# Folding the FFN weight preparation into the first FFN pass, with weights stored block by block, in a Mamba + FFN + attention layer on eight cores

## The chip, the cores and the metric

The kernel runs on the eight cores of one Trainium2 chip. Each core takes one of eight sequences (2048 tokens, 1024 features) and all weights; the cores exchange nothing. The metric is device microseconds of the slowest core. The engines of a core are PE (matmul; PEld is its weight load), DVE (vector), ACT (scalar/activation), POOL (GpSimd) and SP, which here only issues DMAs. SPq and POOLq are the queues on which they are issued.

## What is computed

The reference, cut to its skeleton (`_layernorm` without scale; every block is added to the residual):

```python
x = x + mamba(_layernorm(x))      # in_proj, conv, silu, x_proj, dt, scan over time, out_proj
x = x + ffn(_layernorm(x))
x = x + attn(_layernorm(x))
x = x + ffn(_layernorm(x))        # the same w1, w2, b1, b2 again

def _binarize(w):                 # w1 is [4096, 1024], w2 is [1024, 4096]
    alpha = mean(abs(w), axis=1, keepdims=True)
    return alpha * sign(w)
def ffn(x):
    h = gelu(einsum('bsd,hd->bsh', x, _binarize(w1)) + b1)
    return einsum('bsh,dh->bsd', h, _binarize(w2)) + b2
```

So both FFN calls need the sign of each weight and, for each output feature, the mean of the absolute weights (alpha).

## The kernel before

The residual X stays in SBUF, features on partitions (8 chunks of 128) and tokens along the free dimension. The program is written by hand: a recorder keeps one list of operations for each engine (`r.op`), waits stand in these lists in program order (`r.wait`), `r.drain` lets the engine finish, `r.inc` is a drain and a semaphore increment, and `r.barrier` joins all engines. An engine that waits holds up all that stands behind it in its list.

- **Mamba** (`_mamba`), four quarters of 512 tokens. In quarter 0 `inproj_block` loads each of 32 blocks of in_proj_w by POOL with a cast to bf16 (L443, 128 columns of the matrix, so runs of 512 B), multiplies (L472, 8 matmuls), and SP writes the bf16 block to `ip_bf` in HBM (L448, runs of 256 B). The load of block m waits for the matmuls and for the write of block m-2, which use the same of two buffers. Quarters 1 to 3 load the block from `ip_bf` (L459); of these, the first 16 blocks are placed between the channel groups of the scan before, the last 16 follow the output projection. `do_outproj` does the same with 8 blocks of out_proj_w (L585, L593, L602; matmuls L611, residual add L618). The scan (L712 ACT exponentials, L726 and L750 DVE products, L734 DVE scan) fills most of the stage and isn't touched.
- **Preparation** (`_ffn_prep`), between two barriers. A first pass over w1 (32 blocks of 128x1024, loads L843) and w2 (8 blocks of 128x4096) takes the sums of absolute values on DVE (L847) and scales them (L852) into `al1_t`, `al2_t`. A second pass loads the transposed weights w1T, w2T in column blocks (L872, runs of 512 B), takes the sign on ACT (L879, f32 to bf16) and writes the result to `w1s`, `w2s` in HBM (L885, runs of 256 B).
- **FFN** (`_ffn`, called twice), each time two halves of 1024 tokens. A half is a layer norm (L298 to L343; its sums over features are f32 and bf16 matmuls with a matrix of ones, L308 and L313); then 32 blocks of the first product: load of a w1s block (L925), 16 matmuls (L936), GELU on ACT with alpha as its scale (L943), with two weight buffers and two PSUM pairs; then 8 blocks of the second product: load of a w2s block (L955, 1 MB), 64 matmuls (L966), alpha and bias on DVE (L973), residual add (L980); then a barrier.
- **Attention** (`_attn`): over the 16 heads of one token, in 16 groups of 128 tokens; not touched.

## Time and profile before

| | us |
|---|---|
| Times of two runs | 6597.5 and 6752.1, median 6674.8 |
| The profiled execution | 6606.3 |
| Span of its slowest core (core 6), on which all rows below are | 6604.8 |
| Spans of the other cores | 6568.6 to 6604.1 |
| Mean granted TensorE clock, every core | 0.66 of full speed |

| Stage on core 6 | from | to | us |
|---|---|---|---|
| start, x and first layer norm | 0 | 101 | 101 |
| Mamba, in-projection of quarter 0 | 101 | 248 | 147 |
| rest of Mamba | 248 | 3583 | 3335 |
| preparation of the FFN weights | 3583 | 4094 | 511 |
| FFN, first call, first half | 4094 | 4385 | 291 |
| FFN, first call, second half | 4385 | 4678 | 293 |
| attention | 4678 | 6010 | 1332 |
| FFN, second call, and the store | 6010 | 6605 | 595 |

A profile row gives busy times of each engine; PEclk is the clock that was granted to TensorE, 1.0 being 2.4 GHz and 0.5 being 1.2 GHz. The profile models the ends of matmuls, so a busy PE is not PE at its peak.

### The profile page before, as it was taken

How to read it: one execution, taken by the hardware profiler on the slowest of the kernel's cores; microseconds unless marked ns; L12 is line 12 of the kernel's file. 1: busy time of each engine (PE TensorE's matmuls, PEld its weight loads, DVE VectorE, ACT ScalarE, POOL GpSimd, SP SyncE). 2: the span in 40 equal slices, each digit the busy share in tenths (PEclk: the TensorE clock that was granted, in tenths of full speed). 3: DMA queues.
4: the chain of work that ended last, by engine and by line, in shares of the span. 5: the costliest groups of instructions: out<-in, count | busy, mean ns of one | idle time of the engine just before them, and what ended most of it. 6: DMA issues, size and time to landing. Idle time of an engine off the chain costs nothing.

```text
span 6604.8 us, 35054 instructions; the slowest of 8 cores (6568.6 to 6604.8 us)
## 1 busy us (share of the span) xinstructions
PE 2579.8 (39%) x8941; PEld 937.6 (14%) x9120; DVE 3260.0 (49%) x3060; ACT 1439.0 (22%) x2794; POOL 330.1 (5%) x124
## 2 busy tenths in 40 slices
PE   3333224232242232322222001879543343337978
PEld 1100001000010000100000000334211111113433
DVE  0267783577845778658885300120356556552011
ACT  0133331233322333223331012212110010011120
POOL 0000000000000000000000000000022322220000
PEclk8655557555575555665556555989766666668989
DMA  6500004100020000110002555323300000002414
GB/s 104 84 10 13 2 0 77 34 13 5 0 51 33 11 8 0 32 45 0 0 0 82 188 127 140 67 42 76 56 0 0 0 0 0 0 2 35 79 42 111
DMA packets 691332, 259.70 MB, mean 39 GB/s; under 512 B 614586, under 2 KB 680253, under 8 KB 687552
## 3 DMA queue, kind: packets, MB, share of 16 engines
q1 hardware_dynamic: 627488, 235.25, 14.6%
q0 software_dynamic: 63648, 22.20, 3.1%
q8 instruction: 78, 1.28, 0.1%
q14 instruction: 118, 0.97, 0.1%
HBM read 241.73 MB, written 37.88 MB: 42 GB/s over the span
## 4 chain that ended last, share of the span: by engine, by line
DVE 35%; PE 27%; DMA 12%; ACT 11%; issue 9%; DVEq 4%; POOL 1%; ACTq 1%; SPq 1%; POOLq 0%
DVE AR L734 18%; PE ps L966 7%; PE ps L936 6%; ACT AR L712 5%; DVE AR L1102 4%; PE ps L472 3%; DVEq L58 3%; DVE AR L1138 3%; PE ps L1165 2%; DVE AR L513 2%; DMA AR<-w1T 2%; PE ps L308 2%; PE ps L1069 2%; DMA AR<-w2T 2%; DMA AR<-w 2%
## 5 line engine op out<-in xcount | busy, mean ns | idle before, releaser
L758 PE MATMUL ps<-AR 128*128 128x512 bf16 x1004 | 510.2, 609 | 1945.7 <-DVE AR L750 1945.7
L734 DVE TENSOR_TENSOR_SCAN AR<-AR 128x1024 bf16<-128x1024 f32 x512 | 1173.5, 2292 | 135.4 <-ACT AR L718 124.0
L712 ACT ACTIVATE AR<-AR 128x511 f32<-128x511 f32 x1024 | 675.3, 707 | 1.4 <-issue 1.1
L936 PE MATMUL ps<-AR 128*128 128x512 bf16 x2008 | 455.1, 384 | 127.0 <-DVE AR L343 111.4
L1165 PE MATMUL ps<-AR 128*128 128x512 bf16 x512 | 220.5, 587 | 636.4 <-POOL AR L1151 609.2
L973 DVE TENSOR_SCALAR AR<-ps,AR 128x1024 f32<-128x1024 f32 x32 | 43.0, 1344 | 859.5 <-PE ps L966 859.5
L966 PE MATMUL ps<-AR 128*128 128x512 bf16 x2007 | 445.3, 382 | 16.3 <-DMA AR<-w2s 14.0
L308 PE MATMUL ps<-X,AR 128*128 128x512 f32 x256 | 133.9, 683 | 737.3 <-ACT AR L298 663.9
L750 DVE TENSOR_TENSOR AR<-AR 128x1024 bf16<-128x1024 bf16 x512 | 354.4, 692 | 125.3 <-issue 125.3
L758 PEld LDWEIGHTS ps<-AR 128*128 128x128 bf16 x1024 | 69.8, 104 | 2376.7 <-issue 2376.7
L743 ACT ACTIVATE AR<-AR 128x2 f32<-128x2 bf16 x512 | 105.0, 205 | 1351.3 <-DVEq L63 1351.3
L472 PE MATMUL ps<-AR 128*128 128x512 bf16 x1004 | 319.7, 481 | 160.3 <-DVE AR L343 66.0
L726 DVE TENSOR_TENSOR AR<-AR 128x1022 bf16<-128x1022 bf16 x512 | 351.1, 686 | 10.7 <-issue 10.7
L1151 POOL TENSOR_TENSOR AR<-AR 128x2048 bf16<-128x2048 bf16 x64 | 279.4, 4366 | 969.9 <-DVE AR L1124 878.5
L1138 DVE TENSOR_TENSOR AR<-AR 128x2048 bf16<-128x2048 bf16 x64 | 219.3, 3426 | 188.3 <-PE ps L1165 186.8
L322 DVE TENSOR_TENSOR AR<-AR 128x1024 f32<-128x1024 f32 (+1 forms) x10 | 10.1, 1013 | 590.5 <-ACT AR L318 590.5
L1102 DVE TENSOR_REDUCE AR<-AR 128x32 f32<-128x2048 bf16 x128 | 292.9, 2288 | 9.4
L1095 DVE TENSOR_TENSOR AR<-AR 128x2048 bf16<-128x2048 bf16 x128 | 155.7, 1217 | 250.8 <-ACT AR L1082 250.8
L936 PEld LDWEIGHTS ps<-AR 128*128 128x128 bf16 x2048 | 197.5, 99 | 384.7 <-issue 171.3
L966 PEld LDWEIGHTS ps<-AR 128*128 128x128 bf16 x2048 | 201.4, 98 | 260.2 <-issue 22.4
L943 ACT ACTIVATE AR<-ps,AR 128x1024 bf16<-128x1024 f32 x128 | 154.2, 1205 | 292.8 <-PE ps L936 292.7
L1069 PE MATMUL ps<-AR 128*128 128x512 bf16 x737 | 184.2, 389 | 71.7 <-ACT AR L1082 40.5
(92 smaller groups left out, 2176.2 us busy)
## 6 DMA issues: line engine op xcount, KB each, us to landing
AR<-w1s SPq DMA_DIRECT2D x128, 256.0 KB, 3.0
AR<-w2s SPq DMA_DIRECT2D x32, 1024.0 KB, 7.0
AR<-ip_bf SPq DMA_DIRECT2D x96, 256.0 KB, 2.9
AR<-bc_hbm SPq DMA_DIRECT2D x4, 4096.0 KB, 14.7
AR<-w SPq DMA_DIRECT2D x32, 512.0 KB, 3.4
AR<-w SPq DMA_DIRECT2D x8, 2048.0 KB, 9.3
AR<-w1T SPq DMA_DIRECT2D x32, 512.0 KB, 4.3
AR<-w2T SPq DMA_DIRECT2D x8, 2048.0 KB, 13.9
```

The source lines that it names most:

```text
L472: c = r.op("pe", lambda e, m=m, b=b, k=k: e.matmul(self.bank(4 + b, TQ), wi[b][:, k, :], xn[:, k, :], start=(k == 0), stop=(k == 7)), inc= ...
L712: nbase=nbase: e.activation(out=dec_all[gb][:, n, 1:TQ], in_=dt[b][:, 1:TQ], func=AF.Exp, scale=av[:, dd, nbase + n:nbase + n + 1]))
L726: e.tensor_tensor(out=inp_all[ib][:, :, 1:], in0=vdup[b][:, :, 1:], in1=bbc[:, nbase:nbase + G, 1:], op=ALU.mult))
L734: e.tensor_tensor_scan(out=h_all[hb].rearrange("p a b -> p (a b)"), data0=dec_all[gb].rearrange("p a b -> p (a b)"), data1=inp_all[ib].rea ...
L750: e.tensor_tensor(out=hc_all[hb], in0=h_all[hb], in1=cbc[:, nbase:nbase + G, :], op=ALU.mult), inc="c_ve")["c_ve"]
L758: e.matmul(self.bank(b, TQ), self.ident[:], hc_all[hb][:, n, :], start=(ng == 0 and n == 0), stop=(ng == NG - 1 and n == G - 1)),
L936: e.matmul(self.pair(4 + 2 * b, TH)[:, a:bnd], w1b[b][:, k, :], xn[:, k, a:bnd], start=(k == 0), stop=(k == 7)),
L966: e.matmul(self.pair(0 + 2 * b, TH)[:, a:bnd], w2b[b][:, k, :], hact[:, k, a:bnd], start=(k == 0), stop=(k == 31)),
L1069: e.matmul(self.pair(4)[0:U, ns * 512:(ns + 1) * 512], xn[:, k, m::16], wt[:, k, ns * 512:(ns + 1) * 512], start=(k == 0), stop=False))
L1102: cv = r.op("ve", lambda e, b=b, jg=jg, jb2=jb2: e.reduce_sum(out=sc[b][0:U, :, 2 * jg:2 * jg + 2].transpose([0, 2, 1]), in_=ot[jb2][0:U], ...
L1138: e.tensor_tensor(out=ot[jb][0:U], in0=vm[b][0:U, 2 * jg:2 * jg + 2, :].unsqueeze(2) .broadcast_to([U, 2, 16, 64]), in1=am[b][0:U, :, 2 * ...
L1165: ns=ns: e.matmul(self.bank(2 * b + ns)[0:U, :], self.ident[0:U, 0:U], ot[jb][:, jj, :, :] .rearrange("p a b -> p (a b)") [0:U, ns * 512:( ...
```

## The change

1. `_ffn_prep` is not called any more. The first call of `_ffn` gets `first=True`, and in its first half (`prep`) it does the preparation itself. For each of the 32 blocks of the first product: SP loads the f32 block of w1 into `sg1`; ACT takes the sign into `w1b` (bf16), drains, and takes the absolute value in place; PE forms the alpha of the 128 output features with 8 f32 matmuls whose stationary operand is the 128x128 block of absolute values and whose moving operand is one column of `onesf` (1/1024); SP writes `w1b` to `w1s`; then come the 16 matmuls as before; ACT copies alpha out of PSUM, drains, and does the GELU.
2. The second product takes w2 in half blocks in all halves (16 of 128x2048 where 8 of 128x4096 were; 32 matmuls for each). In the first half of the first call each half block is loaded in f32, goes through sign and absolute value on ACT, 16 f32 one-column matmuls, and a write to `w2s`. After the second half block ACT copies alpha out of PSUM, and DVE waits for that.
3. The host hands over copies of w1, w2, in_proj_w and out_proj_w in which every 128-column block lies contiguously in the order of the SBUF tile (`w1pk`, `w2pk`, `ip_pk`, `op_pk`), and `w1s`, `w2s`, `ip_bf`, `op_bf` are laid out likewise. So each partition's part of a block is one run (in_proj_w 4 KB, `ip_bf` 2 KB, out_proj_w 8 KB, `op_bf` 4 KB, w1 4 KB, w2 8 KB for each half block).
4. The scratch of the FFN layer norm lies on the place of `hact`.

The core of the diff:

```diff
         self._load_x()
         if "mamba" in self.stages:
             self._mamba()
-        if "prep" in self.stages:
-            self._ffn_prep()
         if "ffn1" in self.stages:
-            self._ffn()
+            self._ffn(first=True)
...
                 ddone = r.op("gp", lambda e, m=m, b=b: e.dma_start(
-                    out=wi[b], in_=d["in_proj_w"][:, m * 128:(m + 1) * 128]
-                    .rearrange("(k p) f -> p k f", p=128)),
+                    out=wi[b].rearrange("p a b -> p (a b)"),
+                    in_=d["ip_pk"][m * 128:(m + 1) * 128, :]),
...
         for hh in range(2):
+            prep = first and hh == 0
...
             for m in range(32):
                 b = m % 2
                 if m >= 2:
                     r.wait("sp", "c_pe", mm_done[m - 2])
+                if prep:
+                    if st_done[b]:
+                        r.wait("sp", dsem("sp", b), st_done[b])
+                    ddone = r.op("sp", lambda e, m=m, b=b: e.dma_start(
+                        out=sg1[b].rearrange("p a b -> p (a b)"),
+                        in_=d["w1pk"][m * 128:(m + 1) * 128, :]),
+                         inc=dsem("sp", b), inck=16)[dsem("sp", b)]
+                    r.wait("act", dsem("sp", b), ddone)
+                    ...
+                    r.op("act", lambda e, b=b: e.sign(out=w1b[b],
+                                                      in_=sg1[b]))
+                    r.drain("act")
+                    r.op("act", lambda e, b=b: e.activation(
+                        out=sg1[b], in_=sg1[b], func=AF.Abs))
+                    ab_done[b] = r.inc("act", "c_act")
+                    r.wait("pe", "c_act", ab_done[b])
+                    for k in range(8):
+                        r.op("pe", lambda e, m=m, b=b, k=k: e.matmul(
+                            self.bank(0, 512)[:, m:m + 1], sg1[b][:, k, :],
+                            self.onesf[:, 0:1], start=(k == 0),
+                            stop=(k == 7)))
+                    r.wait("sp", "c_act", ab_done[b])
+                    st_done[b] = r.op(
+                        "sp", lambda e, m=m, b=b: e.dma_start(
+                            out=d["w1s"][m * 128:(m + 1) * 128, :],
+                            in_=w1b[b].rearrange("p a b -> p (a b)")),
+                        inc=dsem("sp", b), inck=16)[dsem("sp", b)]
...
                 mm_done[m] = c["c_pe"]
                 r.wait("act", "c_pe", mm_done[m])
+                if prep:
+                    r.op("act", lambda e, m=m: e.activation(
+                        out=self.al1_t[:, m:m + 1],
+                        in_=self.bank(0, 512)[:, m:m + 1], func=AF.Copy))
+                    r.drain("act")
                 ev_done[m] = r.op("act", ... func=AF.Gelu, scale=self.al1_t[:, m:m + 1], ...
...
             for m in range(8):
+                bm = m % 2
+                for h in range(2):
+                    sb = 2 * m + h
+                    b2 = sb % 2
+                    k0 = 16 * h
+                    if sb >= 2:
+                        r.wait("sp", "c_pe", m2_done[sb - 2])
+                    if prep:
+                        ... load of sg2[b2] from w2pk by SP; ACT waits for it ...
+                        r.op("act", lambda e, b2=b2: e.sign(out=w2h[b2],
+                                                            in_=sg2[b2]))
+                        r.drain("act")
+                        r.op("act", lambda e, b2=b2: e.activation(
+                            out=sg2[b2], in_=sg2[b2], func=AF.Abs))
+                        ab2 = r.inc("act", "c_act")
+                        r.wait("pe", "c_act", ab2)
+                        for k in range(16):
+                            r.op("pe", ... e.matmul(
+                                     self.bank(4, 512)[:, m:m + 1],
+                                     sg2[b2][:, k, :], self.onesf[:, 0:1], ...
+                        r.wait("sp", "c_act", ab2)
+                        ... write of w2h[b2] to w2s by SP ...
+                    for ns in range(nsl):
+                        for k in range(16):
+                            c = r.op("pe", ... w2h[b2][:, k, :], hact[:, k0 + k, a:bnd],
+                    m2_done[sb] = c["c_pe"]
+                r.wait("ve", "c_pe", m2_done[2 * m + 1])
+                if prep:
+                    r.wait("act", "c_pe", m2_done[2 * m + 1])
+                    al2ev[m] = r.op("act", ... Copy of alpha to al2_t, scale=0.25 ...
+                    r.wait("ve", "c_act", al2ev[m])
```

## Rows read from the trace of the kernel before

**Rows 1.** Page: the 40 slices; PE busy and granted clock in tenths.
```profile
PE   3333224232242232322222001879543343337978
...
PEclk8655557555575555665556555989766666668989
```

**Rows 2.** Windows: stretch, its length, busy us (instructions) of each engine, PEclk, DMA share, GB/s.
```profile
core 6: us, PE busy (x) PEld busy (x) DVE busy (x) ACT busy (x) POOL busy (x), PEclk, DMA share, GB/s
...
101.00:238.00 137.00, 82.90 (x231) 28.27 (x236) 0.00 (x0) 18.52 (x30) 25.30 (x29) 0.74 0.83 108
...
4148.00:4264.00 116.00, 112.46 (x496) 49.04 (x507) 0.00 (x0) 38.65 (x32) 0.00 (x0) 0.98 0.30 69
```

**Rows 3.** Timeline: first DMA of the preparation, then the layer norms of the first two FFN halves.
```profile
3583.25 5.81 SPq L843 DMA_DIRECT2D AR<-w  x3
...
4093.93 7.03 ACT L298 ACTIVATE AR<-X 128x8192 bf16<-128x8192 f32 x1 [5.74 <-SPq L63]
...
4384.85 7.03 ACT L298 ACTIVATE AR<-X 128x8192 bf16<-128x8192 f32 x1 [118.05 <-DVEq L63]
```

**Rows 4.** Groups by shape: busy us, mean ns of one, idle before it and its releaser.
```profile
L943 ACT ACTIVATE AR<-ps,AR 128x1024 bf16<-128x1024 f32 x128 | 154.2, 1205 | 292.8 <-PE ps L936 292.7
...
L879 ACT ACTIVATE AR<-AR 128x1024 bf16<-128x1024 f32 x32 | 33.8, 1057 | 370.0 <-DMA AR<-w1T 370.0
...
L879 ACT ACTIVATE AR<-AR 128x4096 bf16<-128x4096 f32 x8 | 28.9, 3618 | 116.5 <-DMA AR<-w2T 116.5
...
L943 ACT ACT_TABLE_LOAD x4 | 5.1, 1283 | 108.2 <-PE ps L936 108.2
```

**Rows 5.** Timeline: two small ACT operations with a drain between them.
```profile
4829.66 0.22 ACT L1117 ACTIVATE AR<-AR 128x16 f32<-128x16 f32 x1 [0.76 <-DVEq L63]
4829.94 0.22 ACT L1120 ACTIVATE AR<-AR 128x16 f32<-128x16 f32 x1
```

**Rows 6.** DMA issues: queue, count, KB of each, median us to landing.
```profile
AR<-ip_bf SPq DMA_DIRECT2D x96, 256.0 KB, 2.9
...
AR<-w SPq DMA_DIRECT2D x32, 512.0 KB, 3.4
AR<-w SPq DMA_DIRECT2D x8, 2048.0 KB, 9.3
AR<-w1T SPq DMA_DIRECT2D x32, 512.0 KB, 4.3
...
AR<-in_proj_w POOLq DMA_DIRECT2D x32, 256.0 KB, 5.0
ip_bf<-AR SPq DMA_DIRECT2D x32, 256.0 KB, 2.6
```

**Rows 7.** Source L308 (durations ns min/median/max), the stretch 73.3:74.4, then the whole span.
```profile
L308 PEld LDWEIGHTS ps<-X,AR x2: 286/310/333, 73.4 to 73.6; 128*128 128x128 f32 x2
...
L308 PEld LDWEIGHTS ps<-X,AR x256: 190/190/338, 73.4 to 6315.4; 128*128 128x128 f32 x128
L308 PE MATMUL ps<-X,AR x256: 592/592/1193, 73.5 to 6315.8; 128*128 128x512 f32 x128
```

**Rows 8.** Timeline of PEld: f32 weight loads, the first two after idleness, two later ones.
```profile
73.44 0.50 PEld L308 LDWEIGHTS ps<-X,AR 128*128 128x128 f32 x2 [73.44 <-issue]
...
4106.03 0.19 PEld L308 LDWEIGHTS ps<-X,AR 128*128 128x128 f32 x1 [0.24 <-issue]
...
4106.45 0.19 PEld L308 LDWEIGHTS ps<-X,AR 128*128 128x128 f32 x1 [0.24 <-issue]
```

**Rows 9.** Timeline of PE: pairs of in-projection blocks in quarter 0.
```profile
214.94 5.00 PE L472 MATMUL ps<-AR 128*128 128x512 bf16 x16 [5.19 <-DMA AR<-in_proj_w]
...
223.99 5.30 PE L472 MATMUL ps<-AR 128*128 128x512 bf16 x16 [4.04 <-DMA AR<-in_proj_w]
```

**Rows 10.** Groups of Mamba's two projections: busy, mean ns, idle before by releaser.
```profile
L472 PE MATMUL ps<-AR 128*128 128x512 bf16 x1004 | 319.7, 481 | 160.3 <-DVE AR L343 66.0 <-DMA AR<-in_proj_w 55.5 <-DMA AR<-ip_bf 30.3
...
L611 PE MATMUL ps<-AR 128*128 128x512 bf16 x501 | 127.2, 412 | 57.5 <-DMA AR<-op_bf 28.9 <-DMA AR<-out_proj_w 25.1 <-DVE X L618 2.9
```

More of the change, by code:

```diff
@@ L132, in _declare_dram @@
         din("w2T", [4 * D, D])
+        din("w1pk", [4 * D, D])
+        din("w2pk", [D, 4 * D])
+        din("ip_pk", [2 * DI, D])
+        din("op_pk", [D, DI])
         din("b1", [4 * D])
@@ L200, in build @@
         if "ffn2" in self.stages:
-            self._ffn()
+            self._ffn(first=False)
         self._store_out()
@@ L448, in inproj_block @@
                 wr_done[m] = r.op("sp", lambda e, m=m, b=b: e.dma_start(
-                    out=d["ip_bf"][:, m * 128:(m + 1) * 128]
-                    .rearrange("(k p) f -> p k f", p=128), in_=wi[b]),
+                    out=d["ip_bf"][m * 128:(m + 1) * 128, :],
+                    in_=wi[b].rearrange("p a b -> p (a b)")),
                      inc=dsem("sp", b), inck=16)[dsem("sp", b)]
@@ L459, in inproj_block @@
                 ddone = r.op("sp", lambda e, m=m, b=b: e.dma_start(
-                    out=wi[b], in_=d["ip_bf"][:, m * 128:(m + 1) * 128]
-                    .rearrange("(k p) f -> p k f", p=128)),
+                    out=wi[b].rearrange("p a b -> p (a b)"),
+                    in_=d["ip_bf"][m * 128:(m + 1) * 128, :]),
                      inc=dsem("sp", b), inck=16)[dsem("sp", b)]
@@ L593, in do_outproj @@
                     o_wr[m] = r.op("sp", lambda e, m=m, b=b: e.dma_start(
-                        out=d["op_bf"][:, m * 128:(m + 1) * 128]
-                        .rearrange("(k p) f -> p k f", p=128), in_=wo[b]),
+                        out=d["op_bf"][m * 128:(m + 1) * 128, :],
+                        in_=wo[b].rearrange("p a b -> p (a b)")),
                          inc=dsem("sp", b), inck=16)[dsem("sp", b)]
@@ L602, in do_outproj @@
                     ddone = r.op("sp", lambda e, m=m, b=b: e.dma_start(
-                        out=wo[b], in_=d["op_bf"][:, m * 128:(m + 1) * 128]
-                        .rearrange("(k p) f -> p k f", p=128)),
+                        out=wo[b].rearrange("p a b -> p (a b)"),
+                        in_=d["op_bf"][m * 128:(m + 1) * 128, :]),
                          inc=dsem("sp", b), inck=16)[dsem("sp", b)]
@@ L889, in _ffn_prep, with _ffn @@
         r.barrier()
-    def _ffn(self):
+    def _ffn(self, first=False):
         T, TH, r, d = self.T, self.TH, self.r, self.dram
@@ new lines, in _ffn @@
+                r.wait("ve", "c_pe", m2_done[2 * m + 1])
+                if prep:
+                    r.wait("act", "c_pe", m2_done[2 * m + 1])
+                    al2ev[m] = r.op("act", lambda e, m=m: e.activation(
+                        out=self.al2_t[:, m:m + 1],
+                        in_=self.bank(4, 512)[:, m:m + 1], func=AF.Copy,
+                        scale=0.25), inc="c_act")["c_act"]
+                    r.wait("ve", "c_act", al2ev[m])
+                r.op("ve", lambda e, m=m, bm=bm: e.tensor_scalar(
+                    out=tmp[bm], in0=self.pair(0 + 2 * bm, TH),
```

129 lines of the change are left out of this document (89 added, 40 removed).

## The prediction

> **What bounds the kernel now.** I read the page's slices first: PE is near full only in the FFN stages, there at nearly full clock; in the slices from 3583 us to 4094 us PE stands still, and before that (Mamba) and in attention it works at two to five tenths [rows 1]. No one engine bounds the kernel; each stage has a chain of its own. The windows show the two stages that the change touches most: the in-projection of quarter 0 has PE busy 60% while the DMA engines are busy 83%, and the first product of an FFN half has PE busy 97% at clock 0.98, so it is PE-bound: 116 us for 32 blocks, 3.6 us each, 3.5 of them 16 matmuls at 2.4 GHz (6.9 at 1.2 GHz) [rows 2]. The timeline gives the length of the preparation: 3583.3 to 4093.9, 510.7 us in which neither Mamba nor the FFN runs [rows 3]. From 4148.0, the start of the first product in the window, to 4384.9, where the next half's layer norm begins, the two products of the first half take 236.9 us [rows 2, 3].
>
> **Removed.** 510.7 us of preparation, all on the path, as barriers stand on both sides; and the present form of the two products of the first half, 236.9 us. Together 747.6 us.
>
> **Added: the new loop of the first product.** Its order on ACT decides. For block m ACT does sign, drain, absolute value, then waits for PE to finish the 16 matmuls, copies alpha, and does the GELU; only then comes the sign of block m+1, and PE can't begin m+1 without the absolute values. So ACT and PE, which overlap today, take turns: two buffers do not help. One turn of ACT is sign 1.06, absolute value 1.06 (taken like the sign, same shape), GELU 1.21 [rows 4], the copy with its drain 0.28 [rows 5], and 0.5 for two more drains and three handovers between engines (estimate; one drain costs 0.06 in [rows 5]): 4.1 us. The load of block m+1 is issued behind the store of m, right after the absolute value of m, so it has all of PE's turn (8 us below) and the GELU to land; it takes 3.4 us in 4 KB runs [rows 6]. It would show only from about 9 us on.
>
> **The alpha matmuls** are what the trace of before doesn't show: f32 with a 128x128 stationary operand and one column. An f32 matmul is two records, each with its own weight load (128 calls in the layer norms give 256 records), so the 256 + 256 new matmuls are 1024 passes. The price p of a pass is bounded so. One f32 weight load alone lasts 0.19 us at full and 0.34 at half clock [rows 7]. Two loads issued together after idleness last 0.29 and 0.33 and both end within 0.50, so the second ends 0.21 after the first: they overlap, and the distance at 1.2 GHz is 0.21 us [rows 7, 8]. Halved for 2.4 GHz it is 0.11. With 512 columns the hot passes follow at 0.42 us, and the record lasts 0.59, 0.17 more; cold 1.19 against twice 0.42, 0.35 more [rows 7, 8]. So the low end is p = 0.11 (hot, loads back to back), the high end is load plus that tail, 0.36 hot and 0.69 cold, if each pass had to wait for the one before, which adds into the same PSUM column. I take the overlapped spacing, as two loads show it, plus 0.03: 0.24 for the 512 passes of the first product, which follow an idle turn of 4 us; 0.20 for the 256 of the first half blocks of w2 and 0.15 for the 256 of the second, which follow PE work: 123 + 51 + 38 = 212 us, mean 0.207.
>
> The Trainium skill ("TensorE: Matmul & The Clock Gate", LDWEIGHTS) puts a weight load at its number of columns over 1.2, 0.107 us for 128, independent of rows. By it 1024 passes would be 110 us and the time some 102 us lower than my sum. The trace agrees only with the hot spacing; its single loads last 0.19 and more.
>
> **The clock.** A burst of PE that follows 4 to 5 us of idleness runs its first part at 1.2 GHz: 16 matmuls took 5.0 and 5.3 us in quarter 0, where hot they take 3.5 [rows 9], so a pause costs 1.6 us. Whether the alpha passes, almost all weight load, already bring the clock up, no row shows. If so the 16 matmuls cost 3.5, if not 5.1; I take 4.3. Likewise a half block of w2 (32 matmuls, 6.9 hot) 6.9 to 8.5, and I take 7.7.
>
> **Sum of the two products.** First: 32 x (4.1 + 4.3) = 269 us without passes. Second: for the second half block of a pair ACT works while PE does the first (sign and absolute value of 128x2048, between 1.06 and 3.62 each [rows 4], so 1.9; with the load of 1 MB, between 3.4 and 9.3 [rows 6], that is 9 to 13 us under PE's 14), but for the first half block ACT waits for PE's last matmul to copy alpha: 0.28 + 3.8 + 0.5 = 4.6 us bare. 8 x (2 x 7.7 + 4.6) = 160. With 4 for entry and last block and 212 for the passes the new products take 645 us. Less 747.6: -103 us.
>
> **Packed blocks.** In quarter 0 a buffer goes load (5.0), then store (2.6), then load again, the store with the matmuls at its side [rows 6]; a pair of blocks takes 9.05 us [rows 9], 9.2 over the 32 blocks (147 us). w in 4 KB runs lands in 3.4 where the same 512 KB of w1T in 512 B runs takes 4.3 [rows 6]. So I take 4.0 for the load, 2.0 for the store and 0.3 for shorter issue on POOL: 7.3 for a pair, -30 us (0 if nothing gets shorter; -48 if both shrink to two thirds, where PE takes over). Of the waits for weights that remain, out_proj_w 25.1, op_bf 28.9 and ip_bf 30.3 [rows 10], I take 16, 10 and 15. In the other three FFN halves only the first load of w2 is bare, now half the size: 3 us each, -8. Together -79 us (0 to -130). The layer-norm scratch and the half blocks of w2 there cost nothing: a 512 KB load of 3.4 us lies under 6.9 us of matmuls; without this cover each of 48 would cost up to 3.4.
>
> The Trainium skill ("DMA: Bandwidth & Descriptors", Specifications) has full rate from 512 B runs on, so the f32 loads would gain nothing and only the bf16 blocks would. Then 33 us of the 79 are lost (16 x 1.3 of quarter 0, and 12) and the time is that much later. The rows of w and w1T speak against it.
>
> Total: -103 - 79 = -182. The profiled execution took 6606.3 us, so **6424 us**. The median of the two runs, 6674.8, is pulled up by one at 6752; the profiled one agrees with the other, 6597.5, and I forecast against it.
>
> In one formula: change = 1024 p - 395 with the half-way clock, -356 if all bursts of PE pay the 1.6, -433 if none does, and -213 if PE stays at 1.2 GHz (32 x (4.1 + 6.9) + 8 x (27.6 + 4.6) + 4 - 827).
>
> **Rivals.**
> - *PE never warms up in the new loops.* It works two thirds of each turn, and Mamba's scan, with PE at two to three tenths, shows a clock of 0.5 to 0.6 [rows 1]; against it, quarter 0 reaches 0.74 at 60% [rows 2]. -213 + 1024 x 0.24 = +33: 6639 us.
> - *Weight loads of the passes don't overlap* because a matmul stands between them: 0.34 cold and 0.26 mixed, 306 us instead of 212: 6518 us.
> - *Each pass waits for the sum of the one before in the same PSUM column.* This is the slower side: 0.67 for 512 passes and 0.5 for the others, 599 us, +204: 6810 us. It decides from a mean of p = 0.39 (no gain) and 0.52 (2% slower). Nothing in the rows excludes it; in the layer norm such sums in one place follow without a gap, but with 512 columns.
> - *The packed blocks bring nothing*, other waits taking the transfers' place: +79: 6503 us.
> - *Absolute value or sign is not in ACT's table for GELU.* Signs ran without a load before, while another table was in place, and each load is 1.28 us [rows 4]. Two for each of 32 blocks: +82: 6506 us.
> - *All hot and back to back*: 1024 x 0.107 - 433 = -323: 6283 us.
>
> **How the numbers follow.** Chances: forecast 0.50, with its own range 6385 (hot bursts) to 6460 (cold starts); PE cold 0.10; loads not overlapped 0.12; sums waiting 0.10; packing without gain 0.08; table loads 0.04; all hot 0.06. A measurement can tell about 2%, 132 us: faster is below 6474, slower above 6738. Faster: the forecast, all hot, and the better third of packing without gain, 0.59. Slower: waiting sums and the PE-cold case with dearer passes, 0.12. Same: 0.29. The range 6300 to 6640 leaves out all hot (0.06) and the sums that wait (0.10), with edges.
>
> **What the profile after would show.** The preparation's lines are gone and the layer norm starts at once after Mamba. In the first FFN half blocks follow every 12 us where they followed every 3.6; ACT and PE alternate there; the alpha matmuls' weight loads stand 0.2 to 0.25 us apart. The second product's pairs take about 32 us (2 x 7.7, 4.6, and 11 of passes). A pair of in-projection blocks in quarter 0 takes 7.3. I am wrong if blocks follow every 15 us or more (passes or clock), if table loads appear beside every GELU, or if ACT waits for w1pk, or if the quarter-0 pairs stay at 9.

## The result, and the profile after

The changed kernel takes 6546.5 us (median of 11 runs, 6500.1 to 6578.2), the kernel before 6661.2 (median of 10, 6590.4 to 6752.1). The ratio is 0.986 with a 95% interval from 0.981 to 0.992. So the change is a gain of 1.4% (0.8 to 1.9), some 91 us, where 182 us were forecast, and lies inside the 2% that I called no change. The profiled execution took 6524.7 us (span 6523.2, core 3; the rows below are on that core unless another is named). Totals are compared without the executions in which one die ran more slowly than the other; that is why the ratio isn't the quotient of the medians.

The slices of the page after, PE and PEclk:

```profile
PE   3333224322242322422224777879434433447978
...
PEclk8665557555575555665556666679766666667989
```

A slice is about 165 us. The hole of three slices in PE (0, 0, 1) is gone, as forecast, and 7, 7, 7, 8, 7 stand where the first FFN half runs now. The digits below them are the news: the clock is 0.6 where PE is busy at 0.7 to 0.8. In [rows 1] and [rows 2] the FFN ran at 0.98. The windows say the same (columns as in [rows 2]; first product of the first half, then the second):

```profile
3604.00:4014.00 410.00, 294.57 (x966) 168.84 (x966) 0.00 (x0) 101.63 (x121) 0.00 (x0) 0.62 0.18 58
4014.00:4330.00 316.00, 262.55 (x1100) 159.00 (x1099) 23.01 (x18) 74.50 (x47) 0.00 (x0) 0.73 0.24 82
```

One block of the first product, in the timeline (start, duration, engine, line, operation; in brackets the idle time before it and what ended it):

```profile
3794.41 3.54 PE L953 MATMUL ps<-AR 128*128 128x1 f32 x16 [3.82 <-ACTq L63]
3794.82 0.33 SPq L938 DMA_DIRECT2D AR<-w1pk  x1
3797.82 6.43 PE L975 MATMUL ps<-AR 128*128 128x512 bf16 x16
3804.35 0.17 ACT L983 ACTIVATE AR<-ps 128x1 f32<-128x1 f32 x1 [10.14 <-PE ps L975]
3804.59 1.20 ACT L987 ACTIVATE AR<-ps,AR 128x1024 bf16<-128x1024 f32 x1
3805.69 1.04 ACT L945 ACTIVATE AR<-AR 128x1024 bf16<-128x1024 f32 x1
3806.80 1.06 ACT L948 ACTIVATE AR<-AR 128x1024 f32<-128x1024 f32 x1
3808.07 3.54 PE L953 MATMUL ps<-AR 128*128 128x1 f32 x16 [3.82 <-ACTq L63]
```

This is the block that the prediction described: PE waits while ACT does alpha, GELU, sign and absolute value, then ACT waits 10.14 us for PE. The load of the next block (L938) is issued early, and no ACT row of this block waits for it. The block takes 13.66 us where 12.2 were forecast: the 16 matmuls last 6.43 us instead of 4.3, that is at 1.2 GHz almost to their end. The passes' busy time in the row, 3.54 for 16, runs into that of the matmuls by 0.13; from start to start they take 3.41, 0.213 each.

Two half blocks of w2, the same view:

```profile
4126.78 6.02 PE L1030 MATMUL ps<-AR 128*128 128x1 f32 x32 [4.39 <-ACTq L63]
4132.67 9.71 PE L1058 MATMUL ps<-AR 128*128 128x512 bf16 x32
...
4142.22 4.39 PE L1030 MATMUL ps<-AR 128*128 128x1 f32 x32
4146.47 9.64 PE L1058 MATMUL ps<-AR 128*128 128x512 bf16 x32
```

Here the second half block is the surprise. PE comes to its passes out of full work, does all 32 in 4.39 us (0.13 each, most at 2.4 GHz), and the 32 matmuls behind them last 9.64 although PE never stood still; at 2.4 GHz they last 6.9 [rows 2]. It is so in seven of the eight pairs on this core; in the other one all 32 passes ran at 2.4 GHz (3.63 us) and so did the matmuls behind them (7.07).

Where the time went, on core 6, the slowest core of before (6604.8 to 6503.5 us; the stages are bounded by the starts of the layer norms, or of the first DMA of the preparation):

| Stage, core 6 | before | after | measured | forecast |
|---|---|---|---|---|
| start and Mamba | 3583.3 | 3543.7 | -39.6 | -71 |
| preparation | 510.7 | 0 | -510.7 | -510.7 |
| FFN, first call, first half | 291.0 | 760.9 | +469.9 | +407.7 |
| the three other FFN halves and the store | 894.0 | 873.2 | -20.8 | -8 |
| attention | 1325.9 | 1325.7 | -0.2 | 0 |
| sum | 6604.9 | 6503.5 | -101.4 | -182 |

(The stage table ahead of the prediction ends attention at 6010; the layer norm of the second FFN call starts at 6003.5, and 1325.9 is counted to there.) Core 6 flatters the change a little: it was the slowest before, and its preparation of 510.7 us was the longest (487 to 508 on the other cores; the mean of all eight is 497). The mean span of the eight cores fell by 84 us, from 6585 to 6502.

### The profile page after: what moved, and what is told of

Read it like the earlier page. It is cut to its first block, busy times and chain, and to the rows that moved or that the text cites. A ratio compares the mean times of both kernels' runs of the same rounds, so it can differ in the third digit from the quotient of the medians.

```text
span 6523.2 us, 37240 instructions; the slowest of 8 cores (6488.0 to 6523.2 us)
## 1 busy us (share of the span) xinstructions
PE 2925.6 (45%) x10144; PEld 1167.8 (18%) x10144; DVE 3179.8 (49%) x2980; ACT 1506.4 (23%) x2890; POOL 313.9 (5%) x124
## 4 chain that ended last, share of the span: by engine, by line
DVE 34%; PE 33%; ACT 11%; issue 9%; DMA 5%; DVEq 4%; ACTq 2%; POOL 1%; SPq 0%; POOLq 0%
DVE AR L735 18%; PE ps L975 8%; PE ps L1058 7%; ACT AR L713 5%; DVE AR L1205 4%; PE ps L474 3%; DVEq L58 3%; DVE AR L1241 3%; PE ps L1268 2%; DVE AR L515 2%; PE ps L310 2%; PE ps L1172 2%; PE ps L953 2%; PE ps L612 1%; ACTq L58 1%
## 5 line engine op out<-in xcount | busy, mean ns | idle before, releaser
L759 PE MATMUL ps<-AR 128*128 128x512 bf16 x1024 | 518.1, 609 | 1938.4 <-DVE AR L751 1938.4
L975 PE MATMUL ps<-AR 128*128 128x512 bf16 x2048 | 555.3, 442 | 85.9 <-DVE AR L345 84.2
L1268 PE MATMUL ps<-AR 128*128 128x512 bf16 x512 | 220.8, 587 | 636.2 <-POOL AR L1254 609.1
L759 PEld LDWEIGHTS ps<-AR 128*128 128x128 bf16 x1024 | 69.9, 105 | 2377.4 <-issue 2377.4
L1058 PE MATMUL ps<-AR 128*128 128x512 bf16 x2048 | 479.9, 399 | 4.7 <-ACT AR L987 4.7
L474 PE MATMUL ps<-AR 128*128 128x512 bf16 x1024 | 308.9, 466 | 149.8 <-DVE AR L345 66.2
L975 PEld LDWEIGHTS ps<-AR 128*128 128x128 bf16 x2048 | 229.1, 114 | 403.1 <-issue 255.8
L1058 PEld LDWEIGHTS ps<-AR 128*128 128x128 bf16 x2048 | 210.5, 103 | 269.5 <-issue 52.4
L1172 PE MATMUL ps<-AR 128*128 128x512 bf16 x768 | 189.0, 390 | 68.1 <-ACT AR L1185 41.0
L987 ACT ACTIVATE AR<-ps,AR 128x1024 bf16<-128x1024 f32 x128 | 154.1, 1204 | 221.4 <-PE ps L975 219.2
L1268 PEld LDWEIGHTS ps<-AR 128*128 128x128 bf16 x512 | 56.2, 125 | 792.6 <-issue 788.8
```

The costliest lines, as they stand in the source:

```text
L474: c = r.op("pe", lambda e, m=m, b=b, k=k: e.matmul(self.bank(4 + b, TQ), wi[b][:, k, :], xn[:, k, :], start=(k == 0), stop=(k == 7)), inc= ...
L759: e.matmul(self.bank(b, TQ), self.ident[:], hc_all[hb][:, n, :], start=(ng == 0 and n == 0), stop=(ng == NG - 1 and n == G - 1)),
L975: e.matmul(self.pair(4 + 2 * b, TH)[:, a:bnd], w1b[b][:, k, :], xn[:, k, a:bnd], start=(k == 0), stop=(k == 7)),
L1058: k0=k0, h=h, a=a, bnd=bnd: e.matmul(self.pair(0 + 2 * bm, TH)[:, a:bnd], w2h[b2][:, k, :], hact[:, k0 + k, a:bnd], start=(h == 0 and k == 0),
L1172: e.matmul(self.pair(4)[0:U, ns * 512:(ns + 1) * 512], xn[:, k, m::16], wt[:, k, ns * 512:(ns + 1) * 512], start=(k == 0), stop=False))
L1268: ns=ns: e.matmul(self.bank(2 * b + ns)[0:U, :], self.ident[0:U, 0:U], ot[jb][:, jj, :, :] .rearrange("p a b -> p (a b)") [0:U, ns * 512:( ...
```

## The experiments

Eleven kernels were run. Whole times are given as ratios to the kernel before on the same chip where there were several runs; where a kernel ran once or twice only durations inside its trace are read, above all the mean length of a block of the first product (from the first GELU to the last of the half, over 31). Hot and cold stand for PE at 2.4 and at 1.2 GHz.

**Which of the two costs the clock, ACT's pause or the passes?** The first kernel has no passes, the second puts them behind the matmuls.

e1_nopass:

```diff
-                    for k in range(8):
-                        r.op("pe", ... e.matmul(self.bank(0, 512)[:, m:m + 1],
-                            sg1[b][:, k, :], self.onesf[:, 0:1], ...
...
-                        in_=self.bank(0, 512)[:, m:m + 1], func=AF.Copy))
+                        in_=self.onesf[:, 0:1], func=AF.Copy))
```

> Leaves out the 512 alpha matmuls (1024 passes) in the first half of the first FFN call and takes a constant for alpha; all else, the turns between ACT and PE too, stays. In the changed kernel a block of the first product takes 13.65 us: 3.8 with PE idle, 3.4 of passes, 6.4 for the 16 matmuls (3.5 at 2.4 GHz). Theory A, the passes are as good as idleness for the clock, so each block's matmuls start after 7.2 us without work that counts: without the passes the pause is 3.8 and the matmuls take about 5.1, as in quarter 0 of Mamba, block 8.9 us. Theory B, the pause in which ACT works keeps PE at 1.2 GHz by itself and the passes only add their own 3.4: matmuls stay at 6.4, block 10.2 us. In the second product theory A has the second half block of a pair at 6.9 us for 32 matmuls (it took 9.6 behind its passes), theory B leaves it at 9.6.

Measured, core 7: PE behind its pause in the first product, and a second half block of w2.

```profile
3708.11 6.28 PE L970 MATMUL ps<-AR 128*128 128x512 bf16 x16 [3.96 <-ACTq L63]
...
4030.67 7.07 PE L1046 MATMUL ps<-AR 128*128 128x512 bf16 x32 [1.86 <-ACTq L63]
```

The next burst starts at 3718.36, 10.25 us later. Without any pass the 16 matmuls take 6.28 us. So in the first product ACT's turn of 4 us is enough to make them about as slow as they are (theory B); the passes add their own 3.41 us, 13.65 - 10.25 = 3.40. In the second product theory A came out: of the eight second half blocks six took 7.07 us, where in the changed kernel seven of eight took over 9. The two longer ones, 9.91 and 8.75, stood behind pauses of 3.33 and 2.29 us (another pause of 2.81 cost nothing); without the passes PE is done sooner and waits for ACT there too. The whole took 6316.8 us.

e2_swap (first product only; the alpha matmuls moved behind the 16 matmuls, which then wait for the sign alone, so that the absolute value is taken under them):

```diff
-                    r.drain("act")
+                    sgn = r.inc("act", "c_act")
...
-                    r.wait("pe", "c_act", ab_done[b])
+                    r.wait("pe", "c_act", sgn)
... the 16 matmuls ...
+                if prep:
+                    r.wait("pe", "c_act", ab_done[b])
+                    ... the 8 alpha matmuls ...
```

> The same work in another order, in the first product only: PE does the 16 matmuls as soon as the sign is there and the alpha passes behind them, while ACT takes the absolute value under the matmuls. The pause of PE shrinks from 3.8 to 2.7 us. Theory A (passes don't bring the clock up, and come last now): matmuls 5.1 or less, passes after them at full or mixed clock 1.7 to 2.5, block 9.5 to 10.3 us where it was 13.65. Theory B (the alternation alone keeps PE cold): 2.7 + 6.4 + 3.4 = 12.5 us.

Measured, core 1:

```profile
3709.30 1.84 PE L978 MATMUL ps<-AR 128*128 128x1 f32 x16
...
3713.96 5.30 PE L970 MATMUL ps<-AR 128*128 128x512 bf16 x16 [2.81 <-ACTq L63]
```

The block takes 10.2 us on the mean instead of 13.6, as theory A had it. The absolute value leaves the path (1.1 us), but 3.4 us are saved: the passes now follow matmuls at full clock and cost 1.84 us instead of 3.41, and behind a pause of 2.81 instead of 3.82 the matmuls cost 5.3. A change of order that moves 1.1 us of work takes 3.4 off the block. The whole took 6430.4 us.

**Is a block the sum of its parts?** The next three kernels change only how long ACT works in its turn of the first product. e3_noabs leaves out the absolute value, e11_abs_shorter takes it of half the block, e10_abs_longer takes that of half the block a second time.

```diff
 # e3_noabs
-                    r.drain("act")
-                    r.op("act", lambda e, b=b: e.activation(
-                        out=sg1[b], in_=sg1[b], func=AF.Abs))
 # e11_abs_shorter
-                        out=sg1[b], in_=sg1[b], func=AF.Abs))
+                        out=sg1[b][:, 0:4, :], in_=sg1[b][:, 0:4, :],
+                        func=AF.Abs))
 # e10_abs_longer
+                    r.drain("act")
+                    r.op("act", lambda e, b=b: e.activation(
+                        out=sg1[b][:, 0:4, :], in_=sg1[b][:, 0:4, :],
+                        func=AF.Abs))
```

> Leaves out the absolute value of ACT in the first product (the passes then sum signed weights, so alpha is something else); ACT's turn is 1.1 us shorter and nothing else changes there. In the changed kernel all blocks but the first few follow at 13.65 us to the hundredth. If the block is the sum of its parts, theories A and B both give 12.5 us (13.65 - 1.1). Theory C, the block length is held by the moment at which the clock rises and not by the sum: the saved 1.1 us is paid back as matmuls at 1.2 GHz, the block stays above 13 us.

> The changed kernel with ACT's turn in the first product 0.43 us shorter (absolute value of half of each block only; the sums for alpha are off). The pause of PE is 3.4 instead of 3.8 us. e3 (pause 2.7) had blocks of 9.8 and 11.2 us in turn, passes half the time at 2.4 GHz. If the block is the sum: 13.2. If the clock holds it: 13.65. If the clock already survives a pause of 3.4 us: 10 to 11.5, as in e3.

> The changed kernel with ACT's turn in the first product 0.6 us longer (the absolute value of half the block is taken once more; the values stay). Block of the changed kernel: 13.65 us, with 6.43 of matmuls, one or two of the 16 at 2.4 GHz. Sum of parts: 14.3 us with the same matmuls or all at 1.2 GHz. If the moment at which the clock rises holds the block: still 13.65, the longer pause made up by more matmuls at 2.4 GHz.

Measured: two blocks in turn of e3 (core 1), one block of e11 (core 1), one block of e10 (core 3; the next passes start at 3723.90).

```profile
3700.88 1.92 PE L950 MATMUL ps<-AR 128*128 128x1 f32 x16 [2.70 <-ACTq L63]
3702.65 5.30 PE L972 MATMUL ps<-AR 128*128 128x512 bf16 x16
3710.65 3.54 PE L950 MATMUL ps<-AR 128*128 128x1 f32 x16 [2.70 <-ACTq L63]
3714.06 5.06 PE L972 MATMUL ps<-AR 128*128 128x512 bf16 x16
```

```profile
3708.09 2.42 PE L954 MATMUL ps<-AR 128*128 128x1 f32 x16 [3.39 <-ACTq L63]
3710.36 6.46 PE L976 MATMUL ps<-AR 128*128 128x512 bf16 x16
```

```profile
3710.24 3.54 PE L957 MATMUL ps<-AR 128*128 128x1 f32 x16 [4.52 <-ACTq L63]
3713.65 5.73 PE L979 MATMUL ps<-AR 128*128 128x512 bf16 x16
```

| ACT's turn against the changed kernel | pause of PE | passes, start to start | matmuls | block, mean |
|---|---|---|---|---|
| +0.7 (e10) | 4.51 | 3.41 | 5.73 | 13.6 |
| 0 (the changed kernel) | 3.82 | 3.41 | 6.43 | 13.6 |
| -0.43 (e11) | 3.39 | 3.41 or 2.27, in turn | 5.0 or 6.5 | 12.1 |
| -1.1 (e3) | 2.70 | 3.41 or 1.77, in turn | 5.1 or 5.3 | 10.3 |

Behind the first few blocks those of e10 and of the changed kernel both follow at 13.65 us.

It is not the sum. In e10 0.7 us of extra work on ACT costs nothing at all: the matmuls take 0.7 us less, more of them running at 2.4 GHz. In the other direction 0.43 us less saves 1.5, and 1.1 less saves 3.3. Theory C, a block length held fixed, fits e10 and fails in e3 and e11; in e11 none of the three lengths that had been written down came out. What the runs show is that the place in the burst at which the clock rises moves when the length of the turn changes. What makes it rise stays open; a model with cold time fixed per burst is refuted (e10 against the changed kernel), and so is one in which the length of ACT's turn adds as it is.

**Do the passes cost the clock by themselves?** e4_pipe takes ACT's turn away from in front of PE in both products: sign and absolute value of block m+1 are done before ACT waits for the matmuls of block m, alpha goes to four PSUM banks in turn, and SP's list follows that order.

```diff
+            def s1(m):     # load m, sign, absolute value, write
...
+            if prep:
+                s1(0)
             for m in range(32):
                 b = m % 2
                 if prep:
                     r.wait("pe", "c_act", ab_done[m])
-                            self.bank(0, 512)[:, m:m + 1], sg1[b][:, k, :],
+                            self.bank(m % 4, 512)[:, m:m + 1], sg1[b][:, k, :],
...
                 mm_done[m] = c["c_pe"]
+                if prep and m < 31:
+                    s1(m + 1)
                 r.wait("act", "c_pe", mm_done[m])
... and s2(sb), the same for the half blocks of w2 ...
```

> Takes the pause away: sign and absolute value of block m+1 stand on ACT before the copy and GELU of block m (half blocks of w2 likewise, before the copy of alpha), the f32 buffer is free for its next load once the passes have read it, and alpha goes to one of four PSUM banks in turn. Same passes, same matmuls. In the first product PE has 1.7 us of passes (0.107 each at 2.4 GHz) and 3.5 of matmuls: theory A, 1.7 us of passes between matmuls is too short to lose the clock, block 5.3 us, 170 us instead of 437. In the second product a half block has 3.4 us or more of passes; theory A has the clock lost behind them, as it was in the changed kernel's second half blocks without any idleness before: 4.4 + 9.6 = 14 us, 224 us for 16 instead of 270. Together about 6200 us in all (6505 less 310), ratio to the kernel before 0.94. Theory B (only idle time of PE costs the clock): second product 16 x 10.3 = 165 us, 6140 us in all. If the passes kept the clock down in the first product too: block 9.8 us, 6345 us.

Measured, core 4: two rows of the first product, four of the second (PE is in matmuls up to the passes), and two windows around the passes at 3890.28 (columns as in [rows 2]).

```profile
3721.96 3.61 PE L985 MATMUL ps<-AR 128*128 128x512 bf16 x16
3723.96 1.06 ACT L947 ACTIVATE AR<-AR 128x1024 bf16<-128x1024 f32 x1 [2.00 <-DMA AR<-w1pk]
```

```profile
3843.68 3.63 PE L1056 MATMUL ps<-AR 128*128 128x1 f32 x32
3847.17 7.07 PE L1081 MATMUL ps<-AR 128*128 128x512 bf16 x32
...
3890.28 4.24 PE L1056 MATMUL ps<-AR 128*128 128x1 f32 x32
3894.38 9.80 PE L1081 MATMUL ps<-AR 128*128 128x512 bf16 x32
```

```profile
3886.00:3893.00 7.00, 7.00 (x46) 4.73 (x44) 0.00 (x0) 2.11 (x2) 0.00 (x0) 0.98 0.35 128
3893.20:3899.90 6.70, 6.70 (x21) 3.12 (x21) 0.00 (x0) 1.51 (x1) 0.00 (x0) 0.50 0.66 218
```

The ratio is 0.948 [0.939, 0.956], four runs. A block of the first product takes 6.7 to 7.0 us on the eight cores instead of 13.6, and many bursts there last 3.6, with passes of 1.84 us right ahead of them. It isn't the 5.3 that was expected: ACT waits for w1pk, which SP loads for m+1 only behind the write of m. The second product takes 203 us (224 were expected). There PE goes from matmul to pass to matmul without a pause, and still, in 11 of the 15 half blocks that follow another in this way, the 32 matmuls take 9.2 to 9.9 us against 6.9; in one they take 8.75, and in three 7.07. The three stand behind passes that ran at 2.4 GHz to their end; on the other cores three to five were like them. In the windows the clock is 0.98 up to 3893.0, into the passes, and 0.50 from 3893.2, while PE is busy in all of both. So the pause is enough in the first product (e1), and in the second most sets of 32 passes cost the clock without any pause. Why some don't stays open.

**Are short passes cheaper than their number says?** e5_pipe_bf16 is e4 with the absolute values rounded to bf16 and a bf16 column of ones.

```diff
-                    out=sg1[b], in_=sg1[b], func=AF.Abs))
+                    out=ab1[b], in_=sg1[b], func=AF.Abs))
...
-                            self.bank(m % 4, 512)[:, m:m + 1], sg1[b][:, k, :],
-                            self.onesf[:, 0:1], start=(k == 0),
+                            self.bank(m % 4, 512)[:, m:m + 1], ab1[b][:, k, :],
+                            self.onesb[:, 0:1], start=(k == 0),
```

> As e4_pipe, with the absolute values written in bf16 to a tile of their own: the alpha matmuls become 512 bf16 passes instead of 1024 f32 ones, and the f32 buffer is free once ACT has read it. The price of a bf16 pass of one column isn't known from the rows (its weight load lasts 0.10 alone at 2.4 GHz, 0.15 at 1.2 GHz): between 0.03 and 0.10. Theory A (the time in passes is what costs the clock): 8 passes take 0.3 to 0.8 us and 16 take 0.5 to 1.6, too short in both products; block of the first product 4.1, half block of the second 7.9: 131 + 126 = 257 us instead of 706, total near 6060 us, ratio 0.92. Theory B gives the same here. If ACT is the bound (copy, GELU, sign, absolute value: 3.8 us for a block of the first product), it isn't lower than 3.8.

Measured, core 1:

```profile
3722.00 0.34 PE L972 MATMUL ps<-AR 128*128 128x1 bf16 x8 [2.74 <-ACTq L63]
3722.20 3.61 PE L991 MATMUL ps<-AR 128*128 128x512 bf16 x16
3727.07 1.06 ACT L953 ACTIVATE AR<-AR 128x1024 bf16<-128x1024 f32 x1 [3.64 <-DMA AR<-w1pk]
3729.67 6.18 PE L991 MATMUL ps<-AR 128*128 128x512 bf16 x16
```

A block's alpha costs 0.34 us instead of 1.8 to 3.5: half the passes, each 0.04 instead of 0.11 or 0.21. The ratio is 0.939 [0.937, 0.942], but the block falls only to 6.5 to 6.8 us (4.1 had been expected), next to nothing below e4, since it is the load that sets it now: ACT waits 2.6 to 3.6 us for w1pk, and behind that pause a burst can be cold again (6.18). The gain is in the second product, 177 us on this core where e4 took 203; 126 had been expected.

**Is it the place of the load in SP's list?** e9_loads_ahead is e5 with the loads issued two blocks ahead; they no longer wait for the passes of the block before in the same buffer, which read the bf16 copy.

```diff
+            def l1(m): ... the load of block m, behind ab_done[m - 2] and the write of m - 2 ...
             def s1(m):
-                ... load of m ...
+                r.wait("act", dsem("sp", b), ld_done[m])
...
                     ... write of m ...
+                if m < 30:
+                    l1(m + 2)
             if prep:
+                l1(0)
+                l1(1)
                 s1(0)
... and the same for the half blocks of w2 ...
```

> As e5_pipe_bf16, but the f32 blocks are loaded two ahead: on SP the load of block m+2 stands right behind the store of m instead of the load of m+1 behind the store of m, so both buffers are in flight. In e5 a block of the first product took 6.74 us, its ACT idle 2.6 to 3.6 of them for w1pk: absolute value, load 3.6, sign, absolute value in one chain. Theory D (that order on SP is what makes the pipelined loop slow, and the clock falls because of the waits it makes): a buffer now goes store 2.1, load 3.6, sign and absolute value 2.2 and handovers, 8.6 for two blocks, 4.3 a block; the second product falls from 11.5 to 7.9 us for a half block. First half 75 + 45 us shorter: about 6080 us, ratio 0.922. Rival: the DMA rate or the ACT turn (3.8) is the bound and the clock stays mixed: block 5.5 or more, 6150 us.

Measured, core 3: two blocks of the first product, and one half block of the second.

```profile
3714.72 3.61 PE L1000 MATMUL ps<-AR 128*128 128x512 bf16 x16
3718.50 0.34 PE L981 MATMUL ps<-AR 128*128 128x1 bf16 x8 [0.17 <-ACTq L63]
3718.70 3.61 PE L1000 MATMUL ps<-AR 128*128 128x512 bf16 x16
```

```profile
3838.48 0.54 PE L1082 MATMUL ps<-AR 128*128 128x1 bf16 x16
3838.89 7.07 PE L1107 MATMUL ps<-AR 128*128 128x512 bf16 x32
```

The ratio is **0.926 [0.917, 0.935]**, 6086.2 us on the median of four: the fastest of all, 7.4% below the kernel before and about 6% below the change as made. The mean block takes 4.91 us on this core (4.6 to 4.9 on the eight), where 4.3 was expected; the best ones take 3.7 to 4.0 (3718.70 - 3714.72 = 3.98), and there PE is what bounds. But ahead of 17 of the 31 later blocks PE still waits 0.4 to 4.1 us for ACT, and ACT, where it was looked at, for w1pk. A half block of w2 takes 7.3 us, at the high clock, where the changed kernel mostly takes 14 to 16 and 4.4 more in every pair. The first FFN half falls from 761 to 345 us and is 54 us longer than the half before the change, which had no preparation in it (291). The nearest of the expected times, 6080 us, was theory D's.

**What are the two halves of the change worth alone?** e6_pack_mamba is the kernel before with in_proj_w, out_proj_w, `ip_bf` and `op_bf` stored block by block; e7_ffn_only is the changed kernel without that; e8_pack_prep has every matrix stored block by block, but the preparation stays a stage of its own.

```diff
 # e6_pack_mamba, against the kernel before (likewise ip_bf, op_bf, out_proj_w)
-                    out=wi[b], in_=d["in_proj_w"][:, m * 128:(m + 1) * 128]
-                    .rearrange("(k p) f -> p k f", p=128)),
+                    out=wi[b].rearrange("p a b -> p (a b)"),
+                    in_=d["ip_pk"][m * 128:(m + 1) * 128, :]),
 # e8_pack_prep, against the kernel before, beside those of e6
-        for wname, sname, nk, nb in (("w1T", "w1s", 8, 32),
-                                     ("w2T", "w2s", 32, 8)):
+        for wname, sname, nk, nb in (("w1pk", "w1s", 8, 32),
+                                     ("w2pk", "w2s", 32, 8)):
```

> The kernel before with only in_proj_w, ip_bf, out_proj_w and op_bf packed; FFN and its preparation as before. The rows of the changed kernel give Mamba 40 us less than before, where 71 was predicted. If this is the layout's effect alone: 6605 - 40 = 6565, ratio 0.994, the in-projection of quarter 0 at 8.2 us for a pair of blocks. If part of it came from lower load of the memory by the other cores' shorter work: ratio above 0.996.

> The changed kernel with in_proj_w, ip_bf, out_proj_w and op_bf laid out as before: the fused preparation and the packed FFN weights alone. By the rows, -510.7 for the preparation, +470 for the new first half, -21 in the other three halves: -62 us, ratio 0.991. With e6_pack_mamba the two ratios should multiply to that of the changed kernel (0.986).

> The packed layouts in all, but the preparation kept as a stage of its own, its second pass reading w1pk, w2pk and writing w1s, w2s in runs of 2 to 16 KB; the FFN halves in their new form without the fused part. It tells what the fusion itself is worth over packing. Before, the second pass took 345 us (32 blocks of w1 at 6.4 us, 8 of w2 at 17); the landings in the changed kernel (3.6 for a w1 block, 2.1 for its store) give at most 3.6 + 1.2 + 2.1 for a buffer, with two buffers some 4 us a block: 130 us, and 12 us for a w2 block: 100. So the preparation would take 165 + 230 = 395 us instead of 511, the first FFN half 285: total 6605 - 40 - 21 - 6 - 116 = about 6420, which would beat the fused kernel by 85 us. Rival: store and load share the DMA engines and one SP queue in which a store holds up the next load until ACT is done, so the pass stays at 300 us or more: total 6500, as the fused one.

Measured: e6 0.991 [0.989, 0.994] where 0.994 was expected, e7 0.993 [0.991, 0.996] where 0.991 was, e8 0.988 [0.985, 0.990]. The first two multiply to 0.985, which is the whole change (0.986). So the fused preparation with the packed w1 and w2 brings 0.7% where 1.7% (-103 and -8 of 6606) had been summed, and Mamba's packed blocks 0.9% where -71 us, 1.1%, had been. And e8 is as fast as the changed kernel: as it is written, the fusion is worth nothing that a simpler change of layout wouldn't bring. In e8 the preparation takes 435 to 457 us on the eight cores instead of 487 to 511, not the 395 expected; its rival, 6500 us in all, came nearer than the 6420 that the sum gave. The second pass over w1, core 1:

```profile
3707.56 1.06 ACT L882 ACTIVATE AR<-AR 128x1024 bf16<-128x1024 f32 x1 [3.95 <-DMA AR<-w1pk]
3708.75 0.33 SPq L888 DMA_DIRECT2D w1s<-AR  x1
3709.23 0.33 SPq L875 DMA_DIRECT2D AR<-w1pk  x1
3712.77 1.06 ACT L882 ACTIVATE AR<-AR 128x1024 bf16<-128x1024 f32 x1 [4.16 <-DMA AR<-w1pk]
```

Two buffers, yet one block follows the other by 5.2 us: SP issues the next load only behind the write, which waits for ACT. It looks like the same knot as in e4 and e5; loads ahead were not tried here.

## Where the prediction held and where it failed

Steps that held:

- **ACT and PE take turns.** The rows above show it; ACT's turn, pause and handovers together, took 3.8 us where 4.1 were taken, and the loads of w1pk (3.6 us in 4 KB runs, below) landed under PE's turn.
- **The price of a pass.** 0.213 us at 1.2 GHz, as the overlap of two loads in [rows 7, 8] had it; 0.24 was taken. At 2.4 GHz 1.84 / 16 = 0.115 (e2), and 0.109 in e4 (3847.17 - 3843.68 = 3.49 for 32). The rivals in which loads don't overlap or sums wait are gone: with either the 16 passes would take 5.4 us or more. The Trainium skill ("TensorE: Matmul & The Clock Gate", LDWEIGHTS) has 0.107 us for a load; the runs agree with it at 2.4 GHz only.
- **No table loads** beside sign and absolute value: L987, the GELU, again has four table loads in the whole program, as before [rows 4], and L945 and L948 none.

None of the signs of being wrong that the prediction named appeared: blocks of 15 us, table loads, waits for w1pk that hold up a block, pairs that stay at 9. The miss came through a term that stayed below all of them.

Steps that failed, on core 3 unless said otherwise:

**1. The clock term, +90 us.** The step that failed is "If so the 16 matmuls cost 3.5, if not 5.1; I take 4.3". They cost 6.43. The upper bound came from the two bursts of [rows 9], 5.0 and 5.3 behind pauses of 4 to 5 us. It wasn't a bound even for quarter 0, where the same trace has bursts of 6.2 to 6.6 us behind pauses of 2.7 to 3.4:

```profile
119.63 6.56 PE L472 MATMUL ps<-AR 128*128 128x512 bf16 x16 [3.37 <-DMA AR<-in_proj_w]
```

And [rows 2], 82.90 us for 231 matmuls, gives 5.7 for 16 as their mean. The same clock entered the second product: for a half block of w2 6.9 to 8.5 was given and 7.7 taken.

The terms of the two products, us, from the starts and pauses in PE's timeline:

| Term | forecast | measured, core 3 | difference |
|---|---|---|---|
| 512 matmuls of the first product | 32 x 4.3 = 138 | 204 | +66.5 |
| 512 matmuls of the second product | 16 x 7.7 = 123 | 147 | +23.4 |
| passes | 212 | 109 + 87 = 196 | -16 |
| turns of ACT | 32 x 4.1 + 8 x 4.6 = 168 | 120 + 31 = 151 | -17 |
| entry, change of product, end | 4 | 9 | +5 |
| sum | 645 | 706 | +61 |

The cheaper passes and shorter turns hid over a third of the error in the clock. The rival "PE never warms up in the new loops" was the nearest in mechanism and had a chance of 0.10. Its price for 16 matmuls was 6.9, near to 6.43, but it priced all of the second product at the low clock too, and its passes at 0.24 with it, which made 6639. Three others come nearer to the measured time, loads of passes that don't overlap (6518), packing without gain (6503) and table loads (6506); what they describe did not happen, so their numbers are chance.

**2. Mamba's packed blocks, +31 us on core 6.** This is the step "So I take 4.0 for the load, 2.0 for the store and 0.3 for shorter issue on POOL: 7.3 for a pair", and the savings on the other three waits. Forecast -30 (quarter 0, in_proj_w), -16 (out_proj_w), -10 (`op_bf`), -15 (`ip_bf`). Measured: quarter 0 went from 149.4 to 129.9 us (-19.5, mean of the six cores whose records are complete), 11 of it idle time of PE (60.2 to 49.4) and the rest shorter bursts (5.4 to 4.9 us for 16 matmuls). For the others the idle time of PE by releaser, mean of the eight cores, gives 25.4 to 18.3 (-7), 29.2 to 18.7 (-10.5) and 31.3 to 23.4 (-8). That is -45, and the stage as a whole got 43.5 us shorter on the mean core. The DMAs did become shorter, as taken (compare [rows 6]):

```profile
AR<-ip_bf SPq DMA_DIRECT2D x96, 256.0 KB, 2.6
...
AR<-w1pk SPq DMA_DIRECT2D x32, 512.0 KB, 3.6
...
AR<-ip_pk POOLq DMA_DIRECT2D x32, 256.0 KB, 4.0
ip_bf<-AR SPq DMA_DIRECT2D x32, 256.0 KB, 2.1
```

4.0 for the load and 2.1 for the write are near to the values of the prediction, 4.0 and 2.0, and POOL's issue fell from 0.88 to 0.53 us. The pair of in-projection blocks nevertheless takes 8.1 us on the mean (129.9 / 16) and not 7.3; on core 3:

```profile
110.23 5.30 PE L474 MATMUL ps<-AR 128*128 128x512 bf16 x16 [2.21 <-DMA AR<-ip_pk]
118.48 1.89 PE L474 MATMUL ps<-AR 128*128 128x512 bf16 x8 [2.95 <-DMA AR<-ip_pk]
```

The pair fell by 1.2 although load, write and issue shrank by 1.8: a pair is not one load and one write behind each other. A burst that now comes after 2.2 us instead of 4 to 5 [rows 9] still takes 5.30. Which link of the chain of POOL, SP and PE takes the rest was not tried. The Trainium skill ("DMA: Bandwidth & Descriptors", Specifications) has 512 B as the smallest transfer at line rate, so by it the f32 loads would gain nothing. They did: those of in_proj_w fell from 5.0 to 4.0 us and those of w1 from 4.3 to 3.6. But the writes beside them went from runs of 256 B to 2 KB in the same change, and no run changes one without the other, so what the run length of the loads alone does isn't shown.

**3. The other FFN halves, -13 us.** Only the first load of w2 was costed (-8); measured -20.8. Core 6, the two products of all four halves, before and then after:

```profile
L936 PE MATMUL ps<-AR 128*128 128x512 bf16 x2008 | 455.1, 384 | 127.0 <-DVE AR L343 111.4 <-DMA AR<-w1s 12.8 <-issue 0.2
L966 PE MATMUL ps<-AR 128*128 128x512 bf16 x2007 | 445.3, 382 | 16.3 <-DMA AR<-w2s 14.0 <-issue 0.2
```

```profile
L975 PE MATMUL ps<-AR 128*128 128x512 bf16 x2002 | 535.2, 434 | 90.8 <-DVE AR L345 84.2 <-issue 4.1 <-DMA AR<-w1s 0.9
L1058 PE MATMUL ps<-AR 128*128 128x512 bf16 x2001 | 472.4, 398 | 10.1 <-issue 3.6 <-ACT AR L987 3.1 <-DMA AR<-w2s 1.6
```

The waits for `w1s` and `w2s` went from 26.8 to 2.5 us. The prediction had a term for those of w2 alone.

On core 6 the first half took 62 us more than forecast, Mamba 31, the other halves 13 earlier: 62 + 31 - 13 = 80 us, the distance between -182 and -101.

The range, 6300 to 6640, held the time; the chance of 0.59 for faster than 2% was too high, since a single term (the clock) decided between the forecast and "same", and its two ends were read from two bursts. The forecast's own range, 6385 to 6460, did not hold it. The wide one held it because it had room for both missed terms, not because they were foreseen.

## What to carry to other kernels

When a change puts two engines in turns on one block, read all bursts of such a stage and not two of them, and price the turn with PE at its low clock from start to end unless a row of the same rhythm shows otherwise. Don't expect a change of the other engine's turn to show one for one: here +0.7 us cost nothing and -1.1 us saved 3.3. Better is not to let them take turns: put the next block's preparation ahead of the wait for this block, and look at the order in which one DMA queue issues a write that waits and the load behind it; here these two, with the short bf16 passes, made -1.4% into -7.4%. Before fusing a stage, measure what the layout of its data alone brings.

## What the runs showed of the hardware

- A one-column f32 matmul with a 128x128 stationary operand is two passes of 0.109 to 0.115 us at 2.4 GHz and 0.213 at 1.2; PEld's row is as long as PE's beside them. In bf16 it is one of 0.04 us (0.34 for eight, 0.54 for sixteen); at 1.2 GHz eight took 0.35 and sixteen 0.57.
- 32 such f32 passes between matmuls, with PE busy in the record all the while, mostly cost the clock: in e4's second product on core 4 the 32 matmuls behind them took 9.2 to 9.9 us in 11 of 15 cases, and 7.07 in three, where the passes had run at 2.4 GHz to their end. With 16 bf16 passes of 0.54 us in their place they took 7.07 in all 15 (e9, core 3).
- In the first product a turn of ACT of 4 us in each block keeps 16 matmuls at 6.3 to 6.4 us, one of 2.7 to 2.8 us at 5.1 to 5.3; 4.5 us, with a block of the same length, at 5.7. So the pause alone doesn't say it.
- In the first product of e9 the granted clock was 0.93 to 0.96 of full speed on seven cores and 0.92 on core 7 between 3600 and 3725 us, with all eight at work on it, and bursts of 16 matmuls took 3.61 us.
